# A delta-rule layer without barriers between its eleven stages, and its last solve placed among the gates of the next stage

## The reference, cut to what matters

```python
def step(S, inp):                       # one token after the other
    qt, kt, vt, at, gkt = inp           # at = kt * gamma * exp(gkt), gkt = log_sigmoid(x @ Wf)
    Sp = S * jnp.exp(gkt)[..., None]
    u = jnp.einsum('bhk,bhkv->bhv', at, Sp) + vt
    S = Sp + jnp.einsum('bhk,bhv->bhkv', kt, u)
    o = jnp.einsum('bhk,bhkv->bhv', qt, S)
    return (S, o)
...
gate = jax.nn.sigmoid(x @ Wg1 @ Wg2)
out = out * gate
mu = jnp.mean(out, axis=-1, keepdims=True)
var = jnp.mean(jnp.square(out - mu), axis=-1, keepdims=True)
out = (out - mu) * jax.lax.rsqrt(var + 1e-05) * norm_w
return out @ Wo
```

## Time and profile before

| | us |
|---|---|
| median of 3 runs | 1835.32 (1829.82 to 1835.4) |
| the profiled execution | 1837.21 |
| its span in the trace | 1835.0 |
| cycle 0 / 1 / 2 | 19.0 / 27.3 / 43.8 |
| cycles 3 to 7, each | 54.1 to 56.7 |
| cycle 8 / 9 / 10 | 49.9 / 38.3 / 27.2 |
| `output_tail`, gates / loop | 19.1 / 57.4 |
| TensorE busy, share of the span | 90% |
| TensorE's granted clock, mean | 0.88 |

### The profile page before, as it was taken

The page is one execution under the profiler, slowest core; times in us unless marked ns, Lnnn a source line. Parts: engine busy times, 40 slices in busy tenths (PEclk is TensorE's granted clock), DMA queues, the critical chain, the costliest instruction groups (busy, mean ns, idle before and its releaser), DMA issues. The chain is left out here.

```text
span 1835.0 us, 49212 instructions
## 1 busy us (share of the span) xinstructions
PE 1648.3 (90%) x21601; PEld 1476.2 (80%) x21601; DVE 1103.2 (60%) x2417; ACT 688.4 (38%) x1436; POOL 333.8 (18%) x331
## 2 busy tenths in 40 slices
PE   8899968999999999999999999776888888766789
PEld 8788756998889999999999999656877777765668
DVE  7677757555454555546455455557566666653885
ACT  6466644332232222223222232253433434333642
POOL 4633335000000000000000000153222222200830
PEclk9999979999999999999999999876666666655899
DMA  6000011000010000001000000100000000001001
GB/s 212 1 2 3 2 49 46 1 24 24 1 47 1 24 24 24 24 1 47 1 24 24 1 1 1 39 1 2 4 3 4 3 3 4 4 4 52 1 12 44
DMA packets 11701, 36.10 MB, mean 20 GB/s; under 512 B 3400, under 2 KB 8032, under 8 KB 8928
## 3 DMA queue, kind: packets, MB, share of 16 engines
q1 hardware_dynamic: 11488, 32.97, 5.2%
HBM read 30.47 MB, written 2.49 MB: 18 GB/s over the span
## 5 line engine op out<-in xcount | busy, mean ns | idle before, releaser
L1126 ACT ACTIVATE hidden<-bank,moe_b 128x512 f32<-128x512 f32 (+1 forms) x320 | 213.3, 668 | 536.8 <-PE bank L1018 524.2
L1035 PE MATMUL bank<-moe_w2h,hidden_hi 128*128 128x256 f32 x1216 | 345.7, 284 | 0.0
L1035 PE MATMUL bank<-moe_w2l,hidden_hi 128*128 128x256 f32 x1216 | 344.0, 283 | 0.0
L1035 PE MATMUL bank<-moe_w2h,hidden_lo 128*128 128x256 f32 x1216 | 344.0, 283 | 0.0
L1160 DVE SCALAR_TENSOR_TENSOR residual<-bank,gates,residual 128x256 f32<-128x256 f32 x152 | 73.4, 484 | 290.4 <-PE bank L1035 290.4
L1018 PE MATMUL bank<-x_hi,moe_w1h 128*128 128x512 f32 (+1 forms) x640 | 243.8, 381 | 2.8 <-ACT hidden L1126 2.8
L1018 PE MATMUL bank<-x_lo,moe_w1h 128*128 128x512 f32 (+1 forms) x640 | 242.5, 379 | 0.0
L1018 PE MATMUL bank<-x_hi,moe_w1l 128*128 128x512 f32 (+1 forms) x640 | 242.0, 378 | 0.0
L1035 PEld LDWEIGHTS bank<-moe_w2h,hidden_hi 128*128 128x128 f32 x1216 | 233.1, 192 | 6.0 <-DVE residual L1160 4.3
L1035 PEld LDWEIGHTS bank<-moe_w2l,hidden_hi 128*128 128x128 f32 x1216 | 233.2, 192 | 1.2
L1035 PEld LDWEIGHTS bank<-moe_w2h,hidden_lo 128*128 128x128 f32 x1216 | 233.2, 192 | 0.0
(11 more groups left out here) (315 smaller groups left out, 3239.8 us busy)
## 6 DMA issues: line engine op xcount, KB each, us to landing
moe_w<-in_moe_w SPq DMA_DIRECT2D x16, 1024.0 KB, 4.8
patches<-in_patches SPq DMA_DIRECT2D x7, 864.0 KB, 6.3
out<-residual SPq DMA_DIRECT2D x19, 128.0 KB, 1.7
ffn_w<-in_ffn_w SPq DMA_DIRECT2D x2, 1024.0 KB, 5.9
att_w<-in_att_w SPq DMA_DIRECT2D x1, 1536.0 KB, 9.4
delta_w<-in_delta_w SPq DMA_DIRECT2D x1, 1280.0 KB
patches<-in_patches SPq DMA_DIRECT2D x6, 144.0 KB, 2.9
tok_w<-in_tok_w SPq DMA_DIRECT2D x6, 128.0 KB, 2.6
```

What stands on the lines that cost most here:

```text
L1035: mm = nc.tensor.matmul(bank[4 + n % 3][:, 0:D], left, right, start=(i == 0), stop=(i == len(passes) - 1))
L1126: nc.scalar.activation(H[:, i % 4, 0:n], bank[i % 4][:, 0:n], ACT.Relu, bias=b1[:, x, f:f + 1]).then_inc(acted, 1)
```

## The change

1. `delta_stage` becomes `delta_layer`, one stage whose engine programs hold all cycles one after the other (`part(c, nxt, z, y)`). The barriers between cycles are gone; the waits count over the cycles, and new ones stand where the barrier had made them needless.
2. PE begins a cycle with `values`, in banks 4, 5, 2, 3 and no longer 2, 3, 4, 5. `values(0)` waits for the decay exponentials of the chunk before, `values(2)` for its last `weigh`. `a_rows` comes after `values`, and then `project(0)`, `first_half(0)`, `first_half(1)`, `project(1)`. On DVE `log_forget` and `values_of(0)` stand ahead of `a_out`; `inverse_row` 1 to 4 come before `silu_of(0)`, 5 to 11 after. On ACT all four `sigmoid_values` come ahead of `sigmoid(0)`.
3. Only cycles 0 to 9 stay in the layer. Cycle 10, the solve of chunk 7, is written into `output_tail` among its gates. The gates use banks 4 and 5, the turned tiles banks 6 and 7 up to tile 9. The second magnitude sum, the thresholds (`scales`) and `low_out` move behind the gates; `scales` is computed in round 3 of the loop. The buffers that the last solve needs are kept at the other end of SBUF, and the gates are kept in the tile that takes the product.

Core of the diff:

```diff
-            for k in range(CHUNKS + 3):
-                delta_stage(nc, psum, bank, b, k - 1 if 1 <= k <= CHUNKS else None, k if k < CHUNKS else None,
-                            k - 2 if 2 <= k < CHUNKS + 2 else None, k - 3 if k >= 3 else None)
+            delta_layer(nc, psum, bank, b, CHUNKS + 2)
...
-VALUE_BANKS = (2, 3, 4, 5)
+VALUE_BANKS = (4, 5, 2, 3)
...
+                def values(p):
+                    if p == 0:
+                        pe.wait_ge(in_hi, HALVES * (c + 1))
+                        pe.wait_ge(in_lo, HALVES * (c + 1))
+                        if c == 0:
+                            pe.wait_ge(g1_lo, len(spans))
+                        else:
+                            pe.wait_ge(d_exp, CB * c)
+                    if p == 2 and c >= 1:
+                        pe.wait_ge(pa_ready, 2 * CB * c)
...
-            a_rows()
-            for p in range(IP):
-                values(p)
-            first_half(0)
-            project(0)
-            first_half(1)
+                for p in range(IP):
+                    values(p)
+                a_rows()
+                project(0)
+                first_half(0)
+                first_half(1)
                 project(1)
...
+            for k in range(stages):
+                part(*roles(k))
```

and in `output_tail`, PE, then DVE:

```diff
+            first_half(0)
+            gates_and_rows(0)
+            first_half(1)
+            gates_and_rows(1)
+            gates_and_rows(2)
+            remainder(0)
+            gates_and_rows(3)
+            remainder(1)
+            gates_and_rows(4)
+            gates_and_rows(5)
+            second_half(0)
+            gates_and_rows(6)
+            second_half(1)
+            gates_and_rows(7)
+            gates_and_rows(8)
             gate(2 * LEAD)
+            output(0)
+            output(1)
...
+            inverses(0)
             for i in range(2):
+                whole_out(i, 0)
+                whole_out(i, 1)
+            magnitude(1)
             for j in range(TILES + 5):
                 if 0 <= j - 1 < TILES:
                     low_gated(j - 1)
+                if j == 2:
+                    for i in range(2):
+                        low_out(i, 0)
+                        low_out(i, 1)
+                if j == 3:
+                    scales()
```

1362 lines of the change are left out of this document (768 added, 594 removed), and 1 row of the table UB.

## The result

| | before | after |
|---|---|---|
| median, us | 1833.42 (4 runs, 1829.82 to 1835.4) | 1805.88 (4 runs, 1804.04 to 1807.7) |
| ratio, with its 95% interval | | 0.9852 [0.9829, 0.9874] |
| span of the profiled execution, us | 1835.0 | 1805.9 |

The account below looks back on a forecast made before the run. PE bounds a cycle to the end of `output`, then DVE. Terms -2.7 - 1.0 - 8.6 + 8.5 - 0.5 - 1.7 - 9.2 = -15.2 us took 1835.3 to 1820.1; overall range 1808 to 1832.

Parts of the forecast that it names:

- A barrier costs its gap on PE: At the cycle boundaries PE's whole gap goes: 8.6 us into cycles 3 to 7, 1.7 each into 8 and 9.
- The clock still rises in the course of `values`: At the start of a cycle the clock rises during `values` as before, and is then spent on `a_rows`.
- The new order costs 1.7 us a cycle: In cycles 3 to 7, from `a_rows` to `project(1)`, a loss between 1.3 and 2.8, taken as 1.7; +8.5 in all.
- The other cycles: Outside cycles 3 to 7: cycle 1 -2.7 us, cycle 2 -1.0, cycle 8 -0.5, cycle 9 -1.7.
- The tail: Last solve among the gates: -11.8 us to the loop's first `project`, +2.6 in the loop, so -9.2.
- (a): In the solve, the high clock outlasts `a_rows`, so the loss shrinks to some 0.2 us a cycle: 1812; chance 0.14.
- (b): In whole cycles, steady PE work keeps the clock up and wins some 4 us each: 1800; chance 0.03.
- (c): In the tail, PE and ACT obstruct each other among the gates, so it gives only 4 us: 1825; chance 0.12.
- (d): At cycle boundaries, another wait of the same size replaces each barrier: 1833; chance 0.10.
- (e): In the solve bursts of cycles 3 to 7, PE starves for instructions, 6.0 us a cycle: 1844; chance 0.06.
- the forecast's own range: For the whole kernel, from -22 us to -9 us, that is 1813 to 1826.
- my signs of being wrong: Cycles 3 to 7 below 52 or above 57 us, or tail loop starting over 40 us after the last solve's first matmul.

Follow-up runs that it names:

- fenced: The changed kernel, its new order and tail kept, with the two all-engine barriers put back behind each of the ten cycles; 1839.9 us, ratio 1.0025.
- old_order: The changed kernel, without barriers and with its new tail, but PE, ACT and DVE follow the earlier order inside a cycle; 1805.5 us, ratio 0.9828.
- spaced: The changed kernel with four matmuls of 304 columns added behind each of the solve's first seven bursts in cycles 8 and 9; 1815.9 us, ratio 0.9894.
- pe_gap: The changed kernel with one wait added on PE, for ACT's copy of the last inverse, ahead of values in cycles 3 to 8; 1821.6 us, ratio 0.9922.
- filled_again: The changed kernel with pe_gap's wait and four matmuls of 288 columns ahead of it, filling PE's idle time in cycles 3 to 8; 1812.4 us, ratio 0.9883.

## Why the prediction failed, step by step

**A barrier costs its gap on PE: the step that failed.** The gaps themselves were right, 1.7 us each, gone with only 0.4 us a cycle more of waiting in the second part. But I priced a barrier by its idle time alone, and put its effect on `values` at nothing. Ahead of `values` the idle time also holds the clock down: `values` took 5.45 us behind a barrier and 3.82 without (fenced and after, means of cycles 3 to 7), 1.6 us in each of five cycles, of the 9.4 us of busy time between those two kernels. The earlier trace rows showed me how late in the cycle the clock was still high, and the earlier trace rows that `a_rows` gains nothing from it; that `values` took 5.15 us at a clock of 0.63 before, and what it takes at 1.00 (3.45 us, as cycle 7 after the change shows), I did not look at.

**The clock still rises in the course of `values`: wrong, in the same place.** I took this as given in the step on the new order. Without the gap it rises at the start of `values` or within 1.5 us. It was indeed spent on `a_rows` after that: `project(0)` and all bursts ran at 0.50.

**The new order costs 1.7 us a cycle: right in sum with barriers, too much without.** From the end of the head to `remainder` it costs 2.8 us, the upper end that I had worked out and not taken. It gives back 1.6 in `values`, once the barrier is gone, and some 1.2 in the rest of the solve, where slow bursts leave 0.69 us of gaps a cycle in place of 1.97; against `old_order` the latter is 0.45. Neither is in my sum. Measured alone the order costs 7.1 us in five cycles with barriers (I said 8.5) and 2.9 without. That 7.1 is so near is partly luck: it is 2.9 us a cycle up to `remainder`, less 0.6 up to the end of `output` and 0.6 behind it, of which I had reckoned with none. The two mistakes are one: I costed barriers and order each against the kernel before, and added. That sum leaves out the part that appears only when both are done. For cycles 3 to 7, in us a cycle, I had -1.7 + 1.7 = 0; it was -1.7 for the gap, +2.8 up to `remainder`, -1.6 in `values`, -1.2 up to the end of `output` and -0.1 in the rest, -1.9 in all.

**The other cycles.** Cycle 1's `values` starts at 1212.6 and not at 1216.2, as predicted. Cycles 0 to 2 gave 2.0 us more than I said. Cycle 8 is 1.2 us longer, not 0.5 shorter. Its `a_out` is uncovered as I had it:

```profile
1555.70 4.08 PE L2101 MATMUL bank<-values,inverse_t 32*19 32x16 f32 x235 [1.32 <-DVE a_rows L2356]
```

but I had forgotten that its `first_half` loses the high clock as well, two bursts in 5.2 us with their gap where they had taken 4.5.

**The tail.** -11.9 in the trace, -8 to -10 by the ratios of two experiments, against -9.2. PE, in order: the last solve's first matmul, the first turn of the loop, the first `project`, and `ternary_ffn`:

```profile
1633.59 2.31 PE L1520 MATMUL bank<-values,inverse_t 32*19 32x16 f32 x128 [1.35 <-PEq L70]
...
1665.09 0.44 PE L1483 MATMUL bank<-ident,normed_tiles 128*128 128x128 f32 x2 [1.80 <-ACT normed_tiles L1605]
...
1669.57 0.58 PE L1496 MATMUL bank<-delta_wh,x_hi 128*128 128x256 f32 x1 [1.64 <-DVE x_lo L1713]
...
1725.78 0.77 PE L2631 MATMUL bank<-x_hi,w_ternary 128*128 128x512 f32 x1 [1.73 <-PEq L70]
```

The first `project` comes 36.0 us after the solve's start; I said 37.4, and the earlier trace rows had 49.2. The loop got 1.3 us longer, not 2.6. Among the gates the same eight bursts that leave 8.0 us of gaps in a cycle of their own leave 0.7, which is what `spaced` shows as well. POOL's last ternary weights end at 1717.9, 7 us ahead of the stage's end; I said 5:

```profile
1717.18 0.73 POOL L1839 TENSOR_TENSOR w_ternary<-is_up,is_down 128x256 fp32r<-128x256 f32 x1
```

**The rivals.** (a) came nearest in time, 1812, but by another way: the clock did not outlast `a_rows`. (b) fell: in cycle 9 of `spaced` PE was busy for 25.65 of 26.07 us and the clock was 0.51. The Trainium skill (TensorE: Matmul & The Clock Gate, Why this matters for your kernels) says that work without idle stretches holds the full clock; that row doesn't bear it out. (c) fell with the tail's size, (d) since no wait of a barrier's size took its place, (e) since the touching bursts leave 0.8 us a cycle and the rest has fewer gaps than before.

**Range and signs.** The lower end of the forecast's own range doesn't follow from its terms: a loss of 1.3 us a cycle, a tail of -11 and the whole gap of cycle 2 make -20.5 and not -22. None of my signs of being wrong appeared: cycles 3 to 7 are 52.0 to 54.3 us long and so above 52, and the tail's loop starts 31.5 us after the last solve's first matmul. Three of the five cycles did leave the 54 us, give or take 1, that I had written. But a sign that asks for the length of a cycle hides two errors of opposite direction, here +1.1 us up to `remainder` and -2.8 in `values` and behind; the time of `values` by itself would have told.

## What to carry to other kernels

Price a barrier by its gap and by what runs first behind it. Here a gap of 1.7 us cost 2.9 us a cycle where work came next whose time follows TensorE's clock, and 2.1 where it was a row of tiny matmuls. When two edits meet at one place, make the sum for both together, best as a table of two by two. Bursts of small matmuls that touch ran slower here than their own length; put the long matmuls that have to be done anyway between them.

## What the runs showed of the hardware

- An idle time of PE of 1.05 us can be enough to keep the clock down behind it: `values` takes 3.4 us or 5.1 to 6.1 behind the same gap (`pe_gap`), and 3.4 to 3.7 when the gap is filled with matmuls (`filled_again`).
- Which of the two it is changes from cycle to cycle within an execution, three of six each in the one profiled. `pe_gap` spreads more (1813.6 to 1827.4 us) than the changed kernel (1804.0 to 1807.7); but so does the filled one (1805.8 to 1821.0), so the spread isn't shown to come from this.
- Being busy doesn't bring the clock up by itself: it was 0.51 in cycle 9 of `spaced` with PE busy for 25.65 of 26.07 us.
- Bursts of small matmuls that touch come at 25.6 ns a matmul where one takes 18.1, with a gap of 1.0 to 1.4 us behind every 128 matmul records and 128 weight loads (cycle 9 of the changed kernel); 18.3 us of long matmuls between them cost 3.1 us (`spaced`).
- 152 matmuls of 19 columns take 5.2 us whatever the clock, in every kernel here; 24 matmuls of 288 columns take 3.4 us at 1.00 and 6.1 at 0.50 (`pe_gap`).
- The layer's first matmul is at 1196.4 to 1200.3 us in the profiled executions of kernels that are the same up to there. Differences of 3 us between kernels can't be put down to an edit from one profile each.
